# Decaying attention: the sums of squares signalled by themselves and read by ScalarE, which also writes the normed input

## The reference

```python
def _layernorm(x, axis=-1, eps=1e-05):
    m = jnp.mean(x, axis=axis, keepdims=True)
    v = jnp.var(x, axis=axis, keepdims=True)
    return (x - m) / jnp.sqrt(v + eps)

def _L0_attn_ref(x, q, k, log_decay, norm_weight, o_w):
    ...
    lam = jax.nn.sigmoid(log_decay)
    def step(S, v_t):
        S = lam[None, :, None, None] * S + kh[None, :, :, None] * v_t[:, :, None, :]
        o_t = jnp.einsum('hd,bhdv->bhv', qh, S)
        return (S, o_t)
    ...
    o = o * jax.lax.rsqrt(jnp.mean(o * o, axis=-1, keepdims=True) + EPS) * norm_weight
    return o @ o_w.T

x = x + _L0_attn_ref(_layernorm(x, axis=-1), ...)
```

## Time and profile before

| what | us |
|---|---|
| median of 3 runs | 1962.32 |
| range of the runs | 1961.99 to 1964.51 |
| the profiled execution, its own time | 1964.35 |
| its span | 1962.2 |
| busy in the span: PE, DVE, ACT, POOL | 1700.4, 1223.2, 1116.5, 616.6 |

### The profile page before, as it was taken

How to read it: one execution, slowest core, us unless ns; L and a number is a source line. 1 busy time by engine, 2 the same in 40 slices (tenths; PEclk the granted TensorE clock), 3 DMA queues, 4 the chain that set the end, 5 groups by cost and what they waited for, 6 DMA issues and landing times. The chain is left out here.

```text
span 1962.2 us, 40701 instructions
## 1 busy us (share of the span) xinstructions
PE 1700.4 (87%) x13407; PEld 1390.9 (71%) x13412; DVE 1223.2 (62%) x4212; ACT 1116.5 (57%) x2552; POOL 616.6 (31%) x783
## 2 busy tenths in 40 slices
PE   6677777779999999999988999999995999999963
PEld 5455555557788888889976877777774777777742
DVE  6689999957311111110107899899964988888756
ACT  2289999932222222222326666566643888888855
POOL 3333232321211111100114666666632122222217
PEclk9889999979999999999999999999997999999985
DMA  3100100025855565647955000000002111111002
GB/s 118 47 26 18 26 24 20 2 76 186 265 184 192 172 199 164 205 160 236 324 173 172 22 22 22 19 15 22 22 1 66 41 34 34 34 34 34 2 1 86
DMA packets 111695, 171.96 MB, mean 88 GB/s; under 512 B 6832, under 2 KB 86576, under 8 KB 110864
## 3 DMA queue, kind: packets, MB, share of 16 engines
q1 hardware_dynamic: 95248, 142.55, 22.1%
q0 software_dynamic: 6480, 17.70, 3.1%
q10 hardware_dynamic: 9776, 9.31, 1.4%
HBM read 143.45 MB, written 26.08 MB: 86 GB/s over the span
## 5 line engine op out<-in xcount | busy, mean ns | idle before, releaser
L1886 ACT ACTIVATE moe_hT<-moe_p_h,lane_a 128x256 f32<-128x256 f32 (+1 forms) x344 | 131.5, 434 | 370.8 <-PE moe_p_h L1828 370.8
L1828 PE MATMUL moe_p_h<-moe_gT,moe_w 128*128 128x256 f32 (+1 forms) x1376 | 255.7, 344 | 0.8 <-issue 0.8
L1838 PE MATMUL moe_p_y<-moe_w,moe_hT 128*128 128x256 f32 x1136 | 252.3, 379 | 0.0
L1828 PEld LDWEIGHTS moe_p_h<-moe_gT,moe_w 128*128 128x128 f32 x1376 | 227.3, 192 | 25.4 <-issue 1.0
L1336 ACT ACTIVATE xb_pr<-xb_sc,xb_nmax 128x256 f32<-128x256 f32 x512 | 221.1, 501 | 38.8 <-DVE xb_nmax L1393 38.7
L1838 PEld LDWEIGHTS moe_p_y<-moe_w,moe_hT 128*128 128x128 f32 x1136 | 212.5, 190 | 27.1
L1393 DVE CUSTOM_DVE_ANT_0 xb_sc<-xb_p_s,xb_neg 128x256 f32<-128x256 f32 x512 | 187.1, 419 | 54.1 <-PE xb_p_s L1202 52.6
L837 ACT ACTIVATE xa_pr<-xa_sc,xa_nmax 128x256 f32<-128x256 f32 (+1 forms) x512 | 204.1, 453 | 17.5 <-DVE xa_nmax L917 17.1
L1718 POOL DMA_INDIRECT moe_gx<-moe_tokens,moe_source_i x71 | 67.5, 951 | 456.0 <-PE moe_p_t L1815 400.1
L2031 DVE TENSOR_TENSOR moe_gy<-moe_p_y,lane_a 128x256 f32<-128x256 f32 x71 | 27.5, 421 | 229.0 <-PE moe_p_y L1838 229.0
L2006 DVE COPY moe_gT<-moe_p_t 128x512 f32<-128x512 f32 (+1 forms) x43 | 25.7, 599 | 231.9 <-PE moe_p_t L1815 231.9
(11 more groups left out here) (343 smaller groups left out, 3436.0 us busy)
## 6 DMA issues: line engine op xcount, KB each, us to landing
moe_w<-in_L_ffn_w_dram SPq DMA_DIRECT2D x86, 1024.0 KB
moe_rows_out<-moe_gy ACTq DMA_DIRECT2D x28, 256.0 KB
xb_kv<-moe_w SPq DMA_DIRECT2D x18, 256.0 KB, 2.1
X<-in_x_dram SPq DMA_DIRECT2D x4, 1024.0 KB, 9.8
xa_ctx<-in_ctx_turned_dram SPq DMA_DIRECT2D x16, 256.0 KB, 3.1
moe_tokens<-moe_XN_s SPq DMA_DIRECT2D x16, 256.0 KB, 2.2
xb_k_in<-xb_kv SPq DMA_DIRECT2D x16, 256.0 KB
xb_v_in<-xb_kv SPq DMA_DIRECT2D x16, 256.0 KB
```

The source lines that it names most:

```text
L1828: last = pe.matmul(p_h[n % 3][:, k * width:(k + 1) * width], w1[:, r, ic, (2 * n + k) * P:(2 * n + k + 1) * P], gT[:, r % 2, ic, 0:width], ...
L1838: last = pe.matmul(p_y[:, t * D:(t + 1) * D], hT[:, hc, t * P:(t + 1) * P], w2[:, r, hc, :], start=(hc == 0), stop=(hc == HC - 1))
L1886: last = act.activation(hT[:, 2 * n + k, 0:width], p_h[n % 3][:, k * width:(k + 1) * width], ACT.Gelu, bias=b1[:, bass.ds(e * HC + 2 * n + ...
```

## The change

Five things change, all in `decay_attention`. TensorE signals `summed` after the four matmuls of the sums, ahead of the product. ScalarE reads the sums (`read_sums`) where VectorE did. ScalarE also writes `xn`, as `rstd * x + shift`, with two Identity operations; VectorE instead computes `shift = -mean * rstd` for both tiles in one small operation (`centre`). `centre(b + 3)` stands where `norm(b + 2)` stood. `add` waits for `y_ready` by itself, and `measure` waits for `normed`, because it overwrites what `centre` and the norm have read.

```diff
                 for t in range(TB):
                     for c in range(DC):
-                        pe.matmul(p_m[s][:, t:t + 1], osq[:, s, c, t * P:(t + 1) * P], ones[:, :],
-                                  start=(c == 0), stop=(c == DC - 1))
+                        last = pe.matmul(p_m[s][:, t:t + 1], osq[:, s, c, t * P:(t + 1) * P], ones[:, :],
+                                         start=(c == 0), stop=(c == DC - 1))
+                last.then_inc(summed, 1)
...
+            def norm(n, s):
+                act.wait_ge(shifted, n + 1)
+                for t in range(TB):
+                    last = act.activation(xn[:, s, t, :], tile_of(X, n, t), ACT.Identity, scale=rstd[:, s, t:t + 1], bias=shift[:, s, t:t + 1])
+                last.then_inc(normed, 1)
+
+            def read_sums(n, s):
+                act.wait_ge(summed, n + 1)
+                act.activation(sum_sq[:, s, :], p_m[s][:, 0:TB], ACT.Copy).then_inc(sum_sq_ready, 1)
+
+            norm(0, 0)
+            norm(1, 1)
             values(0, 0)
             values(1, 1)
             squares(0, 0)
+            norm(2, 0)
+            read_sums(0, 0)
             for b, h, s in far_turns(act):
                 if has_next(b):
                     squares(b + 1, 1 - s)
                 if has_next(b, 2):
                     values(b + 2, s)
+                if has_next(b, 3):
+                    norm(b + 3, 1 - s)
+                if has_next(b):
+                    read_sums(b + 1, 1 - s)
...
-            def norm(n, s):
-                dve.wait_ge(rstd_ready, n + 1)
-                layer_norm_apply(dve, lambda t: tile_of(X, n, t), lambda t: xn[:, s, t, :], aggr[:, s, :, :], rstd[:, s, :], normed)
+            def centre(n, s):
+                wait_alone(dve, stood_v, (rstd_ready, n + 1))
+                dve.scalar_tensor_tensor(shift[:, s, :], aggr[:, s, :, 0], -1.0, rstd[:, s, :], ALU.mult, ALU.mult).then_inc(shifted, 1)
...
             def add(n, s):
                 dve.wait_ge(rms_ready, n + 1)
+                dve.wait_ge(y_ready, n + 1)
...
             measure(0, 0)
             measure(1, 1)
-            norm(0, 0)
-            norm(1, 1)
+            centre(0, 0)
+            centre(1, 1)
+            dve.wait_ge(normed, 1)
             measure(2, 0)
+            dve.wait_ge(normed, 2)
             measure(3, 1)
+            centre(2, 0)
             scan(0, 0)
...
-                if has_next(b, 2):
-                    norm(b + 2, s)
+                if has_next(b, 3):
+                    centre(b + 3, 1 - s)
                 if has_next(b):
                     scan(b + 1, 1 - s)
-                if not (isinstance(b, int) and b == B):
-                    dve.wait_ge(y_ready, b + 1)
-                    dve.tensor_copy(sum_sq[:, s, :], p_m[s][:, 0:TB]).then_inc(sum_sq_ready, 1)
                 if has_next(b, 4):
+                    dve.wait_ge(normed, b + 3)
                     measure(b + 4, s)
```

More of the change, by code:

```diff
@@ L217, in decay_attention @@
         rstd = ph.sb("rstd", [P, 2, TB])
+        shift = ph.sb("shift", [P, 2, TB])
         v = ph.sb("v", [P, 2, DC, S])
@@ L234, in decay_attention @@
         measured, rstd_ready = ph.sem("measured"), ph.sem("rstd_ready")
+        summed, shifted = ph.sem("summed"), ph.sem("shifted")
         var_eps, mean_eps = ph.sem("var_eps"), ph.sem("mean_eps")
         sum_sq_ready, rms_ready = ph.sem("sum_sq_ready"), ph.sem("rms_ready")
-        stood_p = ph.sem("stood_p")
+        stood_p, stood_v = ph.sem("stood_p"), ph.sem("stood_v")
         chain_v, chain_a = ph.sem("chain_v"), ph.sem("chain_a")
```

## The result

| | before | changed |
|---|---|---|
| median, us | 1964.59 (20 runs) | 1957.97 (20 runs) |
| range of the runs | 1960.1 to 1967.38 | 1953.17 to 1962.26 |
| profiled execution: span | 1962.2 | 1955.9 |
| last add of the stage ends | 83.57 | 76.39 |

What follows compares the result with a forecast made beforehand. VectorE was taken as nearly full, in a 4.05 us turn closed through copy, GpSimd, add, norm and scan. Gains of 0.73 at the start, 2.4 over ten turns and 2.7 at the end made 5.85: median 1956.5, range 1952.0 to 1961.5 us.

Steps and rivals of the forecast that it cites:

- Case A: First stage, steady turns: VectorE's freed time becomes a wait for `rstd`; 5.85 us gained in all; chance 0.60.
- the ring: Steady turn: measuring, power on GpSimd, centre, scan, measuring again set the turn at 3.81 us, bounds 3.56 and 3.96.
- start: First stage up to scan(3): scan(3) begins at 27.60 instead of 28.33, 0.73 us gained.
- Ten turns: Steady stretch from scan(3) to scan(13): 0.24 gained a turn, 2.4 us in all.
- End: From scan(13) to the stage's last add: 12.0 instead of 14.72 us, because `rms` is ready before the product ends; gain 2.7.
- Centre ahead of scan(3): Start of the stage, on VectorE: centre was put at 27.52, with scan(3) following at 27.60.
- squares(0): Start of the stage, on ScalarE: the first squares begin at 15.72 instead of 15.12, 0.6 us later.
- power: GpSimd's power for `rstd` in the steady turn: taken as 0.75 us, between 0.69 and 0.81.
- hand-over to centre: From GpSimd's power to centre on VectorE, behind a separate increment: taken as 0.20 us, bounds 0.04 and 0.20.
- Rival E: Steady turns: GpSimd's `rms` operations stop the scan beside them, turn 4.69, net 5.6 us slower, 1968; chance 0.07.
- `rms`: Steady turn: ready 4.0 us after a scan ends, its add due at 4.8, so slack 0.8.
- Rival D: Behind the first stage: later stages give the gain back as moved work meets the lower clock otherwise, near 1962; chance 0.13.

Runs made afterwards that it cites:

- e3: The changed kernel with centre placed behind the scan instead of in front of it; ratio to the kernel before 0.9928, stage 64.79 us.
- e4: The changed kernel with centre waiting for `rstd` itself instead of behind a separate increment; ratio to the kernel before 0.9962, stage 66.82 us.
- e2: The changed kernel with the copy of the sums back on VectorE behind `y_ready`, no `summed`; ratio to the kernel before 0.9998, stage 76.26 us.
- e1: The kernel before with only the sums signalled early and read by ScalarE, norms staying on VectorE; ratio to the kernel before 0.9942, stage 66.80 us.
- e8: The kernel before, traced once more with nothing changed; stage 75.86 us against 75.93 in its first trace.
- e7: The changed kernel, traced once more with nothing altered; stage 69.10 us against 69.07 in its first trace.
- e5: The changed kernel with centre behind the scan and the first two norms back on VectorE; ratio to the kernel before 0.9929, stage 61.75 us.
- e6: The kernel of e3 run once more with nothing altered; stage 62.64 us against 64.79.

## Why the prediction was right

**The rival that holds.** Case A, the freed time turned into a wait for `rstd`, is what the chip does. The idle stands where it was put, and e3 and e4 show that this ring and nothing else sets the turn.

**The terms.** In the order of the sum: start 0.73 forecast, 0.70 measured (20.69 - 19.99). Ten turns 2.4 forecast, 3.55 measured. End 2.7 forecast, 2.61 measured. Together 5.85 against 6.86, and a median 6.6 lower. That the start fits to 0.03 is luck in part. Centre ahead of scan(3) was forecast for 27.52 on the time of the trace before and came at 27.19, because each step of that chain was about 0.3 earlier; then VectorE stood 0.28 without a wait that the profile shows, in both traces of the changed kernel and in e2 (0.29), not in e4. What this idle is stays open. squares(0) came 0.46 later, not 0.6.

**The mis-sized term** is the ring: 3.81 forecast, 3.70 in the mean. The pieces: power 0.75 taken, 0.69 found; hand-over to centre 0.20 taken, 0.15 found; measuring, centre and scan as taken. These make 3.69; one turn in ten took 3.81. The prediction weighed a rule against a row here: by the Trainium skill, "SBUF — State Buffer", "Who interferes with whom", an add with one operand in PSUM does not block GpSimd, and the power should take 0.69; the row with an add and a norm beside it said 0.81. The power took 0.69 beside the add, so the rule was the better guide. That the 0.81 had not been the add's doing shows best in e2, where the power starts 0.42 after its add as in the kernel before (44.78 and 44.36, against 31.37 and 30.95) but no norm follows on VectorE, and takes 0.69. So the norm is what is left to have lengthened it there. It does not always do so: in e1 the norm starts 0.15 after the power, not 0.37, and the power takes 0.69.

**Rival E, the scan stopped by GpSimd.** The new order did bring them together: GpSimd starts at 38.70, inside the scan of 38.49. The scan kept 1.27. GpSimd paid: 0.47 instead of 0.19 and 0.90 instead of 0.69. In e3, where the same two operations run beside centre and measuring, they take 0.19 and 0.69. The same page of the Trainium skill says that the later of such a pair is blocked until the first is through. The traces agree that GpSimd is blocked. Of the two scan instructions in the row of 38.49 the first ends at 39.18 and the second at 39.76. GpSimd's first operation ends with the first of them, at 39.16. It does so for other starts too: in e4 it begins 0.12 later against the scan and takes 0.35, in e1 it begins 0.23 earlier and takes 0.69, and both end 0.01 to 0.02 ahead of the scan instruction. Each power that began inside a scan instruction ends 0.48 to 0.49 behind the end of that instruction. So these operations wait for what is left of the scan instruction; they do not run slower. The order of starts is not the whole rule: in e1 GpSimd begins 0.03 ahead of the scan by the records and is held all the same.

By this rule the scan was not in danger, since by the prediction's own times GpSimd came after the scan had begun; the rule speaks against rival E there, and not for it, as the prediction has it. GpSimd's wait was off the path and cost slack alone. `rms` was forecast ready 0.8 ahead of its add and was ready 0.37 ahead: the sums came 0.3 sooner than forecast, GpSimd was held for 0.49, and the add was due 0.25 sooner.

**What the sum did not say** is that the two halves of the change work against each other. The gain came from taking the copy out of the ring (e1: 9.1). Moving the norm took 0.57 off an engine that, after that, would have been the bound at 3.57, and put a wait of 0.60 in its place, with the ring at 3.69; it also made the start 0.9 longer (19.99 against 19.05). The loss against e1 is 1.33 + 0.94 = 2.27 us.

**Rival D, later stages give it back.** The profiled spans differ by 6.3 where the stages end 7.18 apart. From the end of the stage to the end of the span it takes 1878.6 before, 1882.1 in e8, 1879.5 changed, 1876.6 in e7, and between 1878.3 and 1883.5 in the others, with no order by how early the stage ended; between the two traces before it is 3.5, where e8's expectation allowed 2. So the rest of the program varies by some 3 us either way between executions, and the gain passes through: the ratios give e1 8.6 to 14.1 us for a stage 9.1 shorter, e5 11.0 to 16.9 for 14.2, and e2 between 2.4 less and 1.8 more for one 0.3 longer. The prediction feared that moved work would meet the lower clock otherwise. In every trace the clock falls to its lower level 0.1 to 4.1 us behind the stage's end, so this fall moves with the work. In all, the lower level takes 171 us behind the stage before and 178 in e8, 169 changed and 159 in e7, in the order of those four rests but for one pair 0.9 apart; e4, with 172 and the longest rest, shows that it is not the only cause.

## What to carry to other kernels

Before a piece of work is moved off a full engine, follow what the new, smaller piece waits for: a two-column operation in front of the longest one carries the whole latency of its input into the ring. Ask how long ago that input was made: one place later in the list gave 5.75 us over ten turns here. And try the parts of a change alone, since one may be paying for the other. Before two starts are compared, see where TensorE's slow pace ends in each.

## What was not expected of the hardware

- A wait put on a separate increment ahead of a VectorE operation costs 0.15 after the release, a wait of the operation itself 0.03 (e4).
- Beside a scan, GpSimd's operations on two columns take 0.47 and 0.90 instead of 0.19 and 0.69: they are held until the scan instruction beside them ends; the scan takes 1.27 either way.
- TensorE's first product takes 3.76 and later ones 1.97. The slow pace ended between 21.2 and 23.2 us in nine traces and at 27.7 in one of the two of the same kernel (e3), which cost that execution 2.1 us against the other. The views print a granted clock of 1.00 for this stretch, but the trace has no record of the clock there; the first one stands where the pace changes.
- In seven of the ten traces GpSimd's gap ahead of one power for `rstd` is 0.31 instead of 0.18, once, between 31 and 35 us. Where the ring through `rstd` sets the turn, that turn is 0.13 longer (3.81 against 3.68 in both traces of the changed kernel, 3.70 against 3.57 in e4); in e1, e3, e5 and e6 it costs nothing, one more sign of which kernels that ring holds. The cause of the gap stays open.
